# The D term of a selective scan moved to TensorE by diagonal matrices, in a new order of the surrounding work

## The reference

```
x = silu(causal_depthwise_conv(xz_half, conv_w, conv_b))
dbc = x @ Wx.T                      # delta, B and C
delta = softplus(delta @ Wdt.T + b_dt)
h = exp(delta * A) * h + delta * B * x          # the scan over 1024 tokens, 16 states
y = sum over states of C * h
y = y + Dp * x                      # Dp: one number for each of 512 channels and direction
return y * silu(z)
...
y = (y_forward + y_backward[:, ::-1]) * 0.5     # one z for both directions
return y @ W_out.T
```

## Time and profile before

| | us |
|---|---|
| median of 3 runs | 4774.53 (4771.92 to 4775.93) |
| profiled execution, its own time | 4780.39 |
| its span, from first to last instruction | 4779.1 |
| first scan begins | 104.1 |
| last scan ends | 4464 |
| a way that holds a sequence's end and the next one's D term (the even ones from w = 2) | 281 to 316 |
| an odd way | 232 to 262 |

### The profile page before, as it was taken

How to read it: one execution, slowest core, us unless ns; L and a number is a source line. 1 busy time by engine, 2 the same in 40 slices (tenths; PEclk the granted TensorE clock), 3 DMA queues, 4 the chain that set the end, 5 groups by cost and what they waited for, 6 DMA issues and landing times.

```text
span 4779.1 us, 52822 instructions
## 1 busy us (share of the span) xinstructions
PE 3469.0 (73%) x16720; PEld 2542.9 (53%) x16720; DVE 3977.1 (83%) x4200; ACT 2993.8 (63%) x4276; POOL 3574.2 (75%) x2131
## 2 busy tenths in 40 slices
PE   3466767786777776787677777787777776778766
PEld 1344445664456644665456554566545654567555
DVE  2999998998989888888888888899888988988500
ACT  3455656685657765677566766578655775677433
POOL 2788878977888778868778787888778877887511
PEclk8566777997879887788778978789778987799887
DMA  4231332654335543356425553255433664245344
GB/s 125 82 109 67 112 131 80 193 177 166 124 102 188 174 158 115 121 191 204 144 71 168 180 196 117 102 176 183 164 119 114 202 200 138 84 145 180 120 150 147
DMA packets 362321, 683.24 MB, mean 143 GB/s; under 512 B 32049, under 2 KB 205626, under 8 KB 358074
## 3 DMA queue, kind: packets, MB, share of 16 engines
q1 hardware_dynamic: 349754, 646.29, 41.2%
q0 software_dynamic: 12288, 33.57, 2.1%
HBM read 510.94 MB, written 168.82 MB: 142 GB/s over the span
## 4 chain that ended last, share of the span: by engine, by line
DVE 28%; PE 20%; issue 16%; POOL 14%; ACT 11%; DMA 10%; SPq 1%; DVEq 0%; POOLq 0%; ACTq 0%
DVE h L1254 12%; POOL drive L1787 7%; DVE y L1287 7%; PE h_t L1085 4%; PE side L1230 4%; DVE side L1349 2%; DMA dx_dram<-prep_work 2%; POOL xs_dram L1851 2%; POOL y L1805 2%; PE side L1207 2%; ACT decay L1490 2%; PE side L1148 2%; DMA delta_dram<-prep_work 1%; DMA expert_w<-in_w 1%; PE side L1129 1%
## 5 line engine op out<-in xcount | busy, mean ns | idle before, releaser
L1787 POOL TENSOR_TENSOR drive<-xu,b_row 128x1024 f32<-128x1024 f32 x960 | 2257.8, 2362 | 412.5 <-DVE h L1254 409.1
L1254 DVE TENSOR_TENSOR_SCAN h<-decay,drive 128x1024 f32<-128x1024 f32 x960 | 2189.4, 2281 | 93.3 <-POOL drive L1787 59.5
L1085 PE MATMUL h_t<-ident,h 128*128 128x128 f32 x8192 | 1515.7, 325 | 803.8 <-DVE y L1287 538.1
L1085 PEld LDWEIGHTS h_t<-ident,h 128*128 128x128 f32 x8192 | 1143.9, 167 | 1294.8 <-DVE y L1287 779.6
L1490 ACT ACTIVATE decay<-delta,neg_a 128x1024 f32<-128x1024 f32 x960 | 1071.3, 1117 | 698.8 <-DVE h L1254 655.2
L1287 DVE SCALAR_TENSOR_TENSOR y<-h_t,c_col,y 128x512 f32<-128x512 f32 x1488 | 1075.3, 737 | 196.1 <-PE h_t L1085 193.7
L1805 POOL TENSOR_TENSOR y<-y,scaled 128x512 f32<-128x512 f32 x496 | 630.9, 1272 | 284.0 <-ACT scaled L1521 276.2
L1222 PE MATMUL side<-xn_t,expert_w 128*128 128x128 f32 x2944 | 414.4, 290 | 62.7 <-DMA expert_w<-in_w 20.6
L1230 PE MATMUL side<-expert_w,work 128*128 128x256 f32 x1384 | 383.9, 429 | 56.1 <-issue 26.5
L1222 PEld LDWEIGHTS side<-xn_t,expert_w 128*128 128x128 f32 x2944 | 378.9, 203 | 80.7 <-ACT work L1733 22.3
L1521 ACT ACTIVATE scaled<-h_t,c_col 128x512 f32<-128x512 f32 x496 | 339.9, 685 | 128.3 <-PE h_t L1085 126.4
(11 more groups left out here) (179 smaller groups left out, 4242.5 us busy)
## 6 DMA issues: line engine op xcount, KB each, us to landing
expert_w<-in_w SPq DMA_DIRECT2D x384, 512.0 KB, 4.2
b_row<-b_dram SPq DMA_DIRECT2D x240, 512.0 KB, 4.2
dx_dram<-prep_work SPq DMA_DIRECT2D x64, 512.0 KB, 4.2
delta_dram<-prep_work SPq DMA_DIRECT2D x64, 512.0 KB, 3.4
delta<-delta_dram SPq DMA_DIRECT2D x64, 512.0 KB, 3.7
work<-xs_dram SPq DMA_DIRECT2D x40, 512.0 KB, 4.9
ys_dram<-work SPq DMA_DIRECT2D x40, 512.0 KB, 5.9
xz_dram<-prep_work SPq DMA_DIRECT2D x32, 512.0 KB, 2.7
```

The source lines that it names most:

```text
L1085: t = pe.e.transpose(h_t[i % N_H_T][:, c * P:(c + 1) * P], its_h[:, c, :], ident[:, :])
L1254: dve.e.tensor_tensor_scan(o, a, v, 0.0, ALU.mult, ALU.add).then_inc(scanned, 1)
L1787: op = pool.e.tensor_tensor(drive[:, k % N_DRIVE, :], xu[:, w % 2, c, :], b_row[:, row % N_B_ROW, :], ALU.mult)
```

## The change

The D term is no longer multiplied and added elementwise. Eight 128x128 matrices with D on their diagonal (two directions, four chunks) are made once by ACT (`d_make`), stored in DRAM and loaded for each sequence (`d_load`, 512 KB) into `xn2_t`, a tile that the experts' combine step of the sequence before still reads. `y_turn` multiplies x of both directions by them into a bank, and adds y to it with four plain matmuls by the identity in place of the transposes. ACT copies the bank to SBUF (`y_copy`), and `gate` reads that. x itself is stored straight from `xu`, in one DMA of 2 MB per way (`x_store`), and fetched as 64 pieces of 512 KB (`x_load`). `dx_mul`, `dx_scale`, `dx_add`, `dx_store`, `dx_load`, `dx_half_load` and `y_add` are gone. The diff without the tables:

```diff
@@ x and D in memory
-        dx_buf = [prep_half, xz_pad[:, PAD:PAD + L]]
+        log_parts = xz_pad[:, PAD:PAD + L]
-        dx_half = work[:, 2 * half:2 * half + 2 * BANK].rearrange("p (k t) -> p k t", k=2)
+        x_half = [work[:, 2 * half:2 * half + 2 * BANK].rearrange("p (d t) -> p d t", d=2),
+                  xn2_t[:, 1, :].rearrange("p (d t) -> p d t", d=2)]
+        d_diag = xn2_t[:, 0, :].rearrange("p (d c t) -> p d c t", d=2, c=EC)
@@ pe_program, y_turn
+                    j = s * EC + c
+                    pe.wait_ge(done["d_load"], 16 * nth("d_load", b))
+                    pe.wait_ge(x_in[j % 2], 16 * (b * (NH * EC // 2) + j // 2 + 1))
+                    for d in range(2):
+                        pe.e.matmul(bank[:, :], d_diag[:, d, c, :], x_half_of(b, j % 2)[:, d, :], start=(d == 0),
+                                    stop=False)
...
                     for q in range(QB):
-                        mm = pe.e.transpose(bank[:, q * P:(q + 1) * P], its_y[:, q, c * P:(c + 1) * P], ident[:, :])
+                        mm = pe.e.matmul(bank[:, q * P:(q + 1) * P], y_half_of(b, s)[:, q, c * P:(c + 1) * P], ident[:, :],
+                                         start=False, stop=(q == QB - 1))
@@ dve_program
-                    else:
-                        dve.wait_ge(dx_out[0], 16 * (w + 1) * (EC // 2))
+                    elif w % 2:
+                        dve.wait_ge(done["u_mul"], nth("u_mul", w - 1, EC - 1))
+                        dve.wait_ge(done["delta_store"], 16 * nth("delta_store", w - 1, EC - 1))
...
-                elif piece == "dx_add":
...
-                elif piece == "y_add":
...
@@ act_program
-                elif piece == "dx_mul":
...
-                elif piece == "dx_scale":
...
-                    else:
-                        act.wait_ge(dx_out[1], 16 * (w + 1) * (EC // 2))
+                    elif w % 2 == 0:
+                        act.wait_ge(done["xz_store"], 16 * nth("xz_store", w // 2, EC - 1))
...
+                elif piece == "d_make":
+                    act.wait_ge(ident_set, 2)
+                    for d in range(2):
+                        for c in range(EC):
+                            op = act.e.mul(d_diag[:, d, c, :], ident[:, :], chan_col(d, c, CHAN_D))
+                elif piece == "y_copy":
+                    b, s, c = index
+                    act.wait_ge(done["y_turn"], nth("y_turn", b, s, c))
+                    op = act.e.copy(y_half_of(b, s)[:, :, c * P:(c + 1) * P],
+                                    side[bank_of["y_turn", index]][:, :].rearrange("p (q t) -> p q t", q=QB))
@@ pool_program, u_mul and gate
-                    if d:
-                        pool.wait_ge(done["dx_add"], nth("dx_add", w, c, NH - 1))
-                    else:
-                        pool.wait_ge(done["dx_mul"], nth("dx_mul", w, c))
+                    pool.wait_ge(x_out[d], 16 * (w // 2 + 1))
...
-                    pool.wait_ge(done["y_add"], nth("y_add", b, s, c))
+                    pool.wait_ge(done["y_copy"], nth("y_copy", b, s, c))
@@ sp_program
+                elif piece == "x_store":
+                    w, = index
+                    b, d = divmod(w, 2)
                     sp.wait_ge(done["silu_x"], nth("silu_x", w))
...
+                    sp.e.dma_start(x_dram[b % 2, d].rearrange("c p t -> p c t"), xu[:, d, :, :]).then_inc(x_out[d], 16)
...
                     if s:
-                        sp.wait_ge(done["y_turn"], nth("y_turn", b, 0, EC - 1))
+                        sp.wait_ge(done["gate"], nth("gate", b, 0, EC - 1))
...
+                elif piece == "d_load":
+                    b, = index
+                    if b:
+                        sp.wait_ge(done["comb_mm"], nth("comb_mm", b - 1, TB - 1))
...
+                elif piece == "x_load":
+                    b, j = index
+                    s, c = divmod(j, EC)
+                    for d in range(2):
+                        sp.wait_ge(x_out[d], 16 * (b + 1))
                     if j >= 2:
-                        sp.wait_ge(done["gate"], nth("gate", b, (j - 2) // EC, (j - 2) % EC))
...
+                        sp.wait_ge(done["y_turn"], nth("y_turn", b, (j - 2) // EC, (j - 2) % EC))
+                    else:
+                        if b == LAST:
+                            sp.wait_ge(drive_made, WHOLE)
+                        if b:
+                            sp.wait_ge(done["comb_mm"], nth("comb_mm", b - 1, TB - 1))
```

415 lines of the change are left out of this document (184 added, 231 removed), and 615 rows, old and new, of tables (AT, BANK_USE).

## The result

The changed kernel takes 4611.06 us (median of 4 runs, 4603.53 to 4613.28) against 4773.23 (4 runs of before beside them, 4766.57 to 4775.93): a ratio of 0.9659 with a 95% interval of 0.9643 to 0.9676, so 162 us less. The prediction was 4720 with a range of 4650 to 4800. The sign was right; the time fell short of the range by 39 us.

The account below looks back on a forecast made before the run. It took a chain through four engines, with DVE the fullest, to bound the even ways, and DVE the odd. Terms -5 -86 +26 +0 +10 -1 +0 = -56 us gave 4720, range 4650 to 4800.

Parts of the forecast that it names:

- The new places: Whole order of pieces: moves every wait for h_t, no row tells which way; 0 us, bounds -25 and +25.
- DVE's gain: Even ways: removed dx_add and y_add and half their waits give 12.3 us each, 86 in all; bounds 0 and 125.
- PE's added work: y_turn's 128 added matmuls, 77 us busy; 3.7 per even way reach the path, 26 in all; bounds 0 and 76.
- Plain matmuls for transposes: y_turn: four plain matmuls cost the same as four transposes, 0; at most 4.5 us per way gained.
- x_load, 10: Before y_turn: PE waits for x to load, 1.5 us per sequence, 10 in all; bounds 0 and 40.
- slower: Rival, chance 0.15: y_turn with x_load holds up h_t, 91 us in place of 10, giving 4800.
- Way 0: First way: eight dx_add leave DVE, 5.4 us, of which 5 taken as gain.
- Head: Ahead of the first softplus: a dx_mul and its store leave the chain; -1 us, bounds -3 and +5.
- Tail: Behind the last scan: eight y_turn in place of four, some 8 us more, half scans relieved; 0, bounds -10 and +30.
- the rival of a clock that pays for the change: Even ways, within "more than that": plain matmuls raise PE's granted clock, 4 to 5 us per way, 30 in all, giving 4690.
- PE takes it back: Rival, chance 0.13: PE's added work reaches the path in full, hardly a wait gained; 4770 to 4790, about no change.
- more than that: Rival, chance 0.17: DVE's waits go in full and PE's work hides; -121 us, about 4655.

Follow-up runs that it names:

- the kernel at 4738.36: New form of the D term in the order of before, with 42 x_load placed one to five slots earlier: 4738.36 us, ratio 0.9935 to before.
- The long windows: Changed kernel's places and banks in slots 608 to 796 and 832 to 1052, old order elsewhere: 4749.6 us with old form, 4716.26 with new form and early loads.
- the short windows: Changed kernel's places and banks only around the starts of sequences 3 to 6, old order elsewhere: 4728.72 us with new form and early loads, 4764.02 with old form.
- the simple banks: Changed kernel with its side banks handed out by one simple rule, 207 of 4905 pieces moved: 5058.9 us; old form in the new places under that rule: 5149.58.
- the moved copy: Changed kernel with its 64 y_copy on DVE in place of ACT, at the same places: 4648.21 us, ratio 0.9739 to before.
- the added work: Changed kernel with 128 DVE additions nobody waits for, at the slots where dx_add and y_add used to be: 4783.03 us, ratio 1.0033 to before.
- the first kernel: New form of the D term in the order of before, x_load where dx_half_load stood: 4769.33 us, ratio 0.9998 to before.

## Why the prediction was wrong

The account of the 162 us, in one table. The part of the form is the kernel at 4738.36 against before, the part of the order is after against that kernel. The rows by stretch come from one profiled execution of each kernel.

| part | predicted | measured |
|---|---|---|
| form of the D term, in the 15 full ways | -55 (-5 -86 +26 +10) | -57.3 |
| form, in head, half scans and tail | -1 | +23.4 |
| new places and banks | 0 (-25 to +25) | -134 by the span, -127 to -131 by the medians |
| sum | -56 | -168 by the span, -162 by the medians |

**The step that failed is "The new places. 0; bounds -25 and +25."** The reason given was that no row tells which way they go. That is a reason for a wide range, not for one of 25 us about zero. The runs showed -127 to -134 in its place. The profile did hold the size of what an order could win: 41 us of idle DVE in way 10 and 263 in the seven even ways, of which I had priced 48. Between the kernel at 4738.36 and after, with the same instructions, an even way lost 18.1 us: 1.7 of DVE's busy time and 16.4 of its waits. Sorted by releaser and summed over the seven, DVE waits less for `h_t` by 8.3 us per way, for POOL's drive by 2.9, for ACT's decay by 2.2, for ACT ahead of delta by 2.0 and for PE in the combine by 1.9; for PE in and behind the router it waits 3.2 more. Behind the shorter wait for `h_t` stands a shorter queue on PE: its idle time in front of the products into `side`, which hold up `h_t`, fell from 150.1 to 84.5 us in the seven even ways. PE's busy time fell too, from 226.6 to 216.9 us per even way, for the same products; why was not tested. The long windows show that the gain is not tied to the new form, at least outside the D term's own stretches. Which of the thousands of moved places bring it was not found; the short windows show only that the first 14 scans of an even way are made lighter (PE 84.2 to 77.1 us in way 10), at the price of the scans around them, and the simple banks show that the order of reuse must fit the places.

**DVE's gain, 86.** Right in its busy time (-82.1 for a forecast of -87), and near in its price: 0.81 taken, 0.90 measured by the moved copy and 0.87 by the added work. It can't be read alone from any kernel here. The sum of the loop's terms came out at -57.3 for -55, and that is partly luck: 13.9 of it lie in the odd ways, where I had put nothing, the even ways gave 36.5 where -86 +26 +10 makes 50, and the kernel that shows it has the loads moved, so that the wait which I had priced at 10 is gone.

**PE's added work, 26.** The working was wrong and the size nearly right. The 256 counts of the projection in the earlier trace rows are 128 matmuls of two instructions each, so each product of 128x512 costs two times 0.5 us, and the whole 129 us rather than 77. What reached the path in the old order was 30 us, 4.2 per even way for 3.7 forecast. In the new order it is 0, and 85 for as much again. That the size came near is luck, as it belongs to an order that the change doesn't have. The sign that I named for this term, DVE's wait for `h_t` up by 20 to 30, failed in the same way: it fell by 24.1 in after, and rose by 37.0 (to 230.7) in the old order. The page's +15.5 us on PE in place of +70 to +80 comes from the order, in which most of PE's other groups are shorter; in the old order it was +88 (3557.2 against 3469.0), and +61 with the early loads. A busy time of PE is no fixed sum of prices, so that sign said nothing of the cost.

**Plain matmuls for transposes, 0 "by the rows".** Wrong, as above. It is small here: the 512 instructions of y are busy for 60.2 + 9.3 = 69.5 us where the 256 transposes of before were for 55.6, so 14 us of PE in all, inside the free amount.

**x_load, 10.** In the old order 31, as the rival "slower" had it, though 60 short of its price: 21.2 us stood in front of one group, and placing the load earlier removed it. In the new order about 0: its loads stand 1.4 slots behind the `y_turn` that frees the buffer in the mean, where the first kernel has 3.1.

**Way 0 and the rest of the loop.** Way 0 gave 8.9 for 5. Even ways shrank by 6.1 to 35.9 each, where I said 5 to 12, and odd ways moved by -10.9 to +11.3, where I said under 3. I counted odd lengthening as a sign of failure. Ways 3 and 13 did lengthen, by 11.3 and 6.9, but not by the form: in the kernel at 4738.36 way 3 is only 4.3 longer than before and way 13 is 3.5 shorter.

**Head, -1.** +5.4, just past the end of its range. Little can be read from it, since the kernels with the head of after take between 104.0 and 109.5 us there. **Tail, 0 (-10 to +30).** +16.7, inside the bounds, and past the 10 that I named as its sign; I had worked out +8 from the loads and then dropped it against a relief of the half scans, which didn't come (+0.2). The tail is where the new form loses.

**The clock as a cause.** The granted clock in even ways rose from between 0.74 and 0.78 to between 0.80 and 0.84, less than the 0.85 that I named. In the kernel at 4738.36 it is in that same region (0.79 to 0.85), and its even ways are only 5.2 us shorter than before. Where it is 0.93, with plain matmuls for `h_t`, the kernel is slower. So the rival of a clock that pays for the change falls.

**Signs that held.** ACT fell by 37.8 (forecast 40); DVE by 82; no wait for x over 1 us outside the tail; `u_mul` (POOL) doesn't wait for the stores of x. The rival "PE takes it back" is what the first kernel did, at 4769, and its reason was the late load and PE together. The rival "more than that", at 4655, came nearest to the time, but not by its mechanism: it has the form alone bring 121 us, and in the old order the form brought 31 to 35.

## What to carry to other kernels

Where a change comes with a new order of the work, cost the order as a part of its own and first: the idle time of the fullest engine is what it may bring, and no row bounds it near zero. To split form from order, run the new form in the old order, and put long stretches of the new order into the old form; short ones give their gain back at the seams. To see what an order does, add up the idle time in front of the side work on the engine that all share. An engine with side work has a free amount in it: price the addition by leaving it out and by doubling it, since one of the two alone would have said 0 or the full price here.

## What the runs showed of the hardware

- A plain 32-bit matmul is two instructions on PE, a transpose one. Durations alone hide it (272 ns and 273 ns at least); the count of instructions against the count in the code shows it. In this kernel 128 products of 128x512 cost 1.0 us of PE each.
- A DVE addition of two SBUF operands into SBUF, 64x512, took 687 ns at the least, 1552 in the median and 5696 at most, beside a POOL that was busy for three quarters of the time; `dx_add` with one operand in PSUM took 656 to 694. In 92 of 128 cases its end lay 547 to 555 ns behind the end of a POOL operation. POOL was busy for 38.8 us more in that kernel, too. The Trainium skill has a rule for this ("GPSIMD Engine Reference", the table's row on SBUF interfaces: it shares them with VectorE, with contention where a DVE instruction has two SBUF inputs). The traces agree. The scan, which takes `drive` from SBUF but `decay` from PSUM, took between 2246 and 2297 ns, with no such spread, though over 600 of the 960 whole scans of before began while an elementwise operation of POOL was under way.
- The granted clock rose when transposes became plain matmuls: way 0 has 0.61 with transposes and 0.81 with plain ones, at 132.3 us and 166.8 us of busy PE. Kind and busy time changed together there.
